# A Mamba stage in an eight-stage kernel: gate, norm and softplus moved between engines

## The chip, the cores and the metric

One core of one Trainium2 chip (trn2) runs the whole program in one launch. The metric is the device time of an execution in microseconds. The engines meant here are TensorE (PE, with PEld for its weight loads), VectorE (DVE), ScalarE (ACT), GpSimd (POOL) and SyncE (SP), which mostly issues DMAs. Each has its own queue of instructions and runs it in order; they meet at semaphores.

## The reference

The program is a decoder of four layers on x of shape (4, 256, 256), each layer a cross-attention and a feed-forward block with gated residuals. Only the first block, a Mamba layer, is touched by the change:

```
def _L0_xattn_ref(hidden_states, z, in_proj_w, conv_w, conv_b, x_proj_w, dt_proj_w, dt_proj_b, A_log, D):
    x = einsum('bld,ed->bel', hidden_states, in_proj_w)
    xc = conv_general_dilated(x, conv_w, padding=[(3, 0)], feature_group_count=256)
    x = silu(xc + conv_b[None, :, None])
    dt_low, Bm, Cm = split(einsum('bdl,ed->bel', x, x_proj_w), [8, 24], axis=1)
    dt = softplus(einsum('brl,dr->bdl', dt_low, dt_proj_w) + dt_proj_b[None, :, None])
    A = -exp(A_log)                                  # 256 x 16
    state = state * exp(dt_t[..., None] * A) + (dt_t * u_t)[..., None] * B_t[:, None, :]   # scan over 256 steps
    y_t = einsum('bdn,bn->bd', state, C_t)
    y = (y + D[None, :, None] * x) * silu(z)
    return swapaxes(y, 1, 2)

x = x + tanh(g_xattn[0]) * _L0_xattn_ref(ctx_1024, _layernorm(x), ...)
x = x + tanh(g_ffn[0]) * _L0_ffn_ref(_layernorm(x), ...)
...
```

So the gate z is the layer norm of x, and the block's result is added to x, of which the next norm is taken for the dense feed-forward block.

## The kernel before

The 1024 tokens are eight tiles (t, NT = 8) of 128 tokens for everything that has tokens on the partitions (X, xn, gate), and two halves (h) of 512 tokens for everything that has channels on the partitions. There are 256 inner channels, two chunks (c, NI = 2) of 128. The state has 16 components; one component of one half is a unit s (UNITS = 32: units 0 to 15 are half 0, 16 to 31 half 1).

Each engine's program is written out by hand, one function for each engine (`mamba_pe`, `mamba_act`, `mamba_dve`, `mamba_pool`, `mamba_sp`); the order in the function is the order in the engine's queue. `tick` and `at` name the semaphore value of an event: an instruction ticks it, others wait for it.

Ahead of the loop: VectorE makes the convolution's weights (L707) and the statistics of x (`bn_stats`, `bn_aggr`, and a small add, "var", L232), for tiles 0 to 3 and then 4 to 7. GpSimd makes 1/sqrt of them by a power (`deviation_pool`, L239), behind a large cast (`sel`, L401). TensorE runs the convolution of half 0 (L440), ScalarE its silu, U (L556), TensorE the projection (L451), ScalarE copies its lowest rows (`low`, L563), TensorE makes dt (L460) and ScalarE and VectorE the softplus: ScalarE Abs (L570), Exp (L575), Ln (L579), VectorE relu (L661), 1 + e (L666), the remainder of that rounding (L671), V minus it (L674), the sum (L679, "DT") and the product with U (L682, "DU"). Meanwhile VectorE splits the projection's rows into three bf16 parts (`split`).

In the loop, each unit s: TensorE spreads a row of B and one of C over the partitions (`rows_of`, L475), ScalarE copies C (L605), in odd units B as well (L601), and makes dA = exp(A dt) into PSUM (L610); VectorE multiplies DU by B (L728; in odd units GpSimd does chunk 1, L410) and scans (L735); GpSimd multiplies the scan by C (L418), and TensorE adds that into y (`add`, L481). One-off work is put behind certain units by `if s == ...` in each engine's loop: half 1's convolution (units 0 to 3) on TensorE; the norms of x, xn (`norm_dve`, L246), on VectorE behind units 0 and 1; silu of half 1 and the gate (L617) on ScalarE at unit 4; the split behind units 6 and 7; half 1's softplus in units 8 to 11; tanh at 11; gating, transposing and adding the first half's result in units 17 to 19; the statistics for the dense stage (tag "d") behind 19, their power on GpSimd in unit 20, the norms on VectorE behind 21, their transposes (`turn_pe`, L258) in 22 and the copies (`turned_act`, `turned_dve`) in 23. The dense stage (L807) starts when TensorE is through with Mamba.

An activation of another function set needs an ACT_TABLE_LOAD; `table_act` runs a dummy activation so that the load comes early. `deviation_dve` and `norm_dve` serve other stages too. GpSimd's loop is:

```
    for s in range(m.UNITS):
        if s + 1 < m.UNITS and shared_out(s + 1):
            ...  # multiply for unit s + 1, chunk 1
        for c in range(m.NI):
            ...  # HC(s, c)
        if s == 20:
            deviation_pool(k, "d", 0)
```

## Time and profile before

| | |
|---|---|
| median of 3 runs | 1137.84 us (1134.45 to 1142.14) |
| profiled execution | 1136.88 us, span 1135.6 us |
| instructions in the span | 14899 |
| busy: PE / DVE / ACT / POOL | 949.6 / 730.4 / 519.2 / 300.4 us |
| chain that ended last | PE 59%, DVE 15%, ACT 3% of the span |
| mean granted TensorE clock | 0.925 of full speed |

The profiled execution is one run, and its span is measured from its first to its last instruction; 1.28 us lie around it. Busy time says how much an engine did, not whether it held up others: for that one reads the chain, or the wait that ended last at a place. Mamba takes the first 174 us of the span.

### The profile page before, as it was taken

How to read it: one execution, taken by the hardware profiler on the slowest of the kernel's cores; microseconds unless marked ns; L12 is line 12 of the kernel's file. 1: busy time of each engine (PE TensorE's matmuls, PEld its weight loads, DVE VectorE, ACT ScalarE, POOL GpSimd, SP SyncE). 2: the span in 40 equal slices, each digit the busy share in tenths (PEclk: the TensorE clock that was granted, in tenths of full speed). 3: DMA queues.
4: the chain of work that ended last, by engine and by line, in shares of the span. 5: the costliest groups of instructions: out<-in, count | busy, mean ns of one | idle time of the engine just before them, and what ended most of it. 6: DMA issues, size and time to landing. Idle time of an engine off the chain costs nothing.

```text
span 1135.6 us, 14899 instructions
## 1 busy us (share of the span) xinstructions
PE 949.6 (84%) x4834; PEld 679.5 (60%) x4834; DVE 730.4 (64%) x1864; ACT 519.2 (46%) x1330; POOL 300.4 (26%) x281
## 2 busy tenths in 40 slices
PE   5677679999999999999997798865878788976556
PEld 2222234668999998888975576733545555544445
DVE  5899994335666668687665346557677855567653
ACT  3574461136666665665632343443356542132331
POOL 3477791131111112143105204341222100010110
PEclk9887899999999999999999799987789999989678
DMA  8400001011111172113004246220100003211100
GB/s 313 201 1 0 1 0 46 1 42 29 43 43 33 43 260 98 43 63 100 11 20 168 74 139 195 94 89 15 43 1 1 1 2 134 74 40 38 70 19 19
DMA packets 28356, 73.96 MB, mean 65 GB/s; under 512 B 4076, under 2 KB 5366, under 8 KB 27640
## 3 DMA queue, kind: packets, MB, share of 16 engines
q1 hardware_dynamic: 24344, 63.28, 16.2%
q0 software_dynamic: 3072, 8.39, 2.3%
q10 hardware_dynamic: 864, 1.34, 0.3%
q8 instruction: 40, 0.66, 0.2%
q14 instruction: 36, 0.29, 0.1%
HBM read 50.98 MB, written 22.02 MB: 64 GB/s over the span
## 4 chain that ended last, share of the span: by engine, by line
PE 59%; DVE 15%; ACT 3%; issue 3%; another core or an unknown queue 2%; POOL 1%; SPq 1%; DMA 1%; DVEq 0%; POOLq 0%; ACTq 0%
PE psum L2042 5%; PE psum L946 5%; PE psum L1652 4%; PE psum L1138 4%; PE psum L1149 4%; PE psum L807 4%; PE psum L1118 4%; PE psum L949 3%; PE psum L1666 2%; PE psum L1129 2%; DVE arena L2338 2%; PE psum L818 2%; PE psum L970 2%; PE psum L2061 2%
## 5 line engine op out<-in xcount | busy, mean ns | idle before, releaser
L1028 POOL TENSOR_TENSOR arena<-arena,mhalf 128x8 f32<-128x8 f32 x32 | 53.7, 1678 | 258.5 <-DVE arena L1013 258.5
L1250 DVE SCALAR_TENSOR_TENSOR X<-psum,arena,X 128x256 f32<-128x256 f32 x128 | 55.9, 478 | 66.7 <-PE psum L1149 64.5
L418 POOL TENSOR_TENSOR arena<-arena 128x512 f32<-128x512 f32 x64 | 83.5, 1331 | 7.4 <-DVE arena L735 4.2
L735 DVE TENSOR_TENSOR_SCAN arena<-psum,arena 128x512 f32<-128x512 f32 x64 | 74.6, 1207 | 3.3 <-ACT psum L610 1.8
L1192 ACT ACTIVATE arena<-psum,arena 128x256 f32<-128x256 f32 x128 | 60.0, 477 | 34.9 <-DVE arena L1229 34.7
L481 PE MATMUL psum<-arena,ident 128*128 128x512 f32 x128 | 72.3, 690 | 1.1 <-POOL arena L418 0.8
L1652 PE MATMUL psum<-arena 128*128 x248 | 66.4, 391 | 7.4 <-DVE arena L1747 4.0
L1758 DVE COPY arena<-psum 128x256 f32<-128x256 f32 x62 | 26.2, 422 | 64.5 <-PE psum L1666 55.3
L1149 PE MATMUL psum<-arena 128*128 128x256 f32 x256 | 65.9, 380 | 1.2 <-DVE X L1250 1.1
L1138 PE MATMUL psum<-arena 128*128 128x256 f32 x256 | 66.5, 383 | 0.0
L2323 ACT ACTIVATE arena<-psum,arena 128x240 f32<-128x240 f32 x128 | 57.4, 465 | 19.1 <-DVE arena L2343 14.6
L1118 PE MATMUL psum<-arena 128*128 128x256 f32 x256 | 65.8, 380 | 0.0
L946 PEld LDWEIGHTS psum<-arena,xT 128*128 128x128 f32 x512 | 62.0, 192 | 1.5
L946 PE MATMUL psum<-arena,xT 128*128 128x128 f32 x512 | 62.3, 275 | 0.0
L2042 PE MATMUL psum<-xT,arena 128*128 128x512 f32 x128 | 60.8, 615 | 1.3 <-ACT arena L3095 1.2
L239 POOL TENSOR_TENSOR rstd<-rstd,mhalf 128x4 f32<-128x4 f32 x16 | 16.3, 1019 | 164.3 <-DVE rstd L232 164.2
L475 PE MATMUL psum<-arena 96*128 96x512 bf16 x64 | 22.4, 436 | 41.7 <-DVE arena L728 41.5
L984 ACT ACTIVATE arena<-psum 128x512 f32<-128x512 f32 x64 | 38.3, 598 | 35.9 <-PE psum L946 17.8
L1204 ACT COPY arena<-psum 128x512 f32<-128x512 f32 x64 | 37.6, 588 | 34.5 <-PE psum L1129 34.4
L1118 PEld LDWEIGHTS psum<-arena 128*128 128x128 f32 x256 | 48.2, 190 | 6.6 <-issue 0.3
L1652 PEld LDWEIGHTS psum<-arena 128*128 128x128 f32 x248 | 43.1, 194 | 14.2 <-issue 10.8
L1149 PEld LDWEIGHTS psum<-arena 128*128 128x128 f32 x256 | 46.3, 190 | 7.0 <-issue 1.4
(348 smaller groups left out, 2282.5 us busy)
## 6 DMA issues: line engine op xcount, KB each, us to landing
arena<-in_w SPq DMA_DIRECT2D x32, 384.0 KB
tokens<-arena SPq DMA_DIRECT2D x2, 4096.0 KB, 23.0
arena<-tokens SPq DMA_DIRECT2D x32, 256.0 KB
results<-arena SPq DMA_DIRECT2D x32, 256.0 KB
arena<-in_moe SPq DMA_DIRECT2D x17, 384.0 KB, 3.0
arena<-in_moe SPq DMA_DIRECT2D x4, 1536.0 KB, 13.8
arena<-in_w SPq DMA_DIRECT2D x2, 1024.0 KB, 6.6
arena<-in_gu SPq DMA_DIRECT2D x1, 1280.0 KB, 5.9
```

Source lines behind the costliest of these rows:

```text
L418: nc.gpsimd.tensor_tensor(m.HC[:, v, :], m.Hs[:, v, :], m.Cs[:, s % 2, :], ALU.mult).then_inc(*tick("HC", s, c))
L481: nc.tensor.matmul(bank[m.bank_Y[h][c]], k.ident[:, :], m.HC[:, 2 * (s % 2) + c, :], start=False, stop=n == NSTATE - 1).then_inc(*tick("y_ ...
L735: nc.vector.tensor_tensor_scan(m.Hs[:, 2 * (s % 2) + c, :], bank[m.bank_dA[c]], input_of(m, s, c), 0.0, ALU.mult, ALU.add).then_inc(*tick( ...
L946: mm = nc.tensor.matmul(bank[b][:, j * P:(j + 1) * P], k.xT[:, c, t * P:(t + 1) * P], m.W[:, p, c * P:(c + 1) * P], start=c == 0, stop=c = ...
L1118: mm = nc.tensor.matmul(bank[w][:, j * S:(j + 1) * S], m.Q[:, N % 2, i * S + j * P:i * S + (j + 1) * P], m.K[:, N % 2, i * S:(i + 1) * S], ...
L1138: mm = nc.tensor.matmul(bank[4][:, 0:S], m.ctok[:, 2 * m.batch(u) + c, :], m.PT[:, u % 2, c, :], start=c == 0, stop=c == 1)
L1149: mm = nc.tensor.matmul(bank[5][:, j * D:(j + 1) * D], m.Z[:, u % 2, j * P:(j + 1) * P], m.M[:, h, :], start=True, stop=True)
L1192: e = nc.scalar.activation(m.Pr[:, w, j, :], bank[w][:, j * S:(j + 1) * S], ACT.Exp, bias=m.nb[:, w, j:j + 1], scale=m.SCALE, accum_out=m. ...
L1250: a = nc.vector.scalar_tensor_tensor(k.X[:, t, :], bank[5][:, j * D:(j + 1) * D], m.ri[:, u % 4, j:j + 1], k.X[:, t, :], ALU.mult, ALU.add)
L1652: mm = nc.tensor.matmul(bank[b][:, 0:D], m.xgT[:, n % 2, c, :], m.W[:, bass.ds(place + c * D, D)], start=c == 0, stop=c == DC - 1)
L2042: mm = nc.tensor.matmul(bank[b], m.W[:, slot, which, c * P:(c + 1) * P], k.xT[:, c, cols], start=c == 0, stop=c == DC - 1)
L2323: nc.scalar.activation(pr[:, a, 0:KM], v[:, a, 0:KM], ACT.Exp, bias=m.nb[:, u, a:a + 1], scale=m.SCALE, accum_out=m.sums[:, a % 2, places[ ...
```

## The change

- ScalarE makes the gate straight from X, tile by tile, silu(x * rstd + shift) with shift = -mean * rstd, in the start: six tiles between the two silus of half 0 and two behind them. VectorE's eight norms behind units 0 and 1 go. The statistics of all eight tiles are finished in one go; GpSimd's power is on 8 columns and stands ahead of its large cast.
- The next norm (tag "d", tiles 0 to 3) is made by ScalarE behind units 21 and 22 from a `shift` that VectorE makes behind unit 20; transposes and copies move from 22 and 23 to 24 and 25.
- The rectification of softplus moves from VectorE to ScalarE (Relu).
- Exp and Ln are used from one table set, loaded once behind `low` and once behind half 1's silu. Tanh moves from unit 11 to the very start, with the DMAs of `ident` and `rows` ahead of those of the projection weights.
- Softplus works chunk by chunk; in half 0 the remainder of chunk 1 is made by GpSimd in three instructions. Half 1's steps are spread over units 8 to 14.

```diff
 # constants_act
     nc.scalar.dma_start(k.cols[:, :], k.io["cols"]).then_inc(*landed("cols_in"))
+    nc.scalar.dma_start(k.ident[:, :], k.io["ident"]).then_inc(*landed("ident_in"))
+    nc.scalar.dma_start(k.rows[:, :], k.io["rows"].partition_broadcast(P)).then_inc(*landed("rows_in"))
     nc.scalar.dma_start(m.Wx, k.io["x_proj"]).then_inc(*landed("Wx_in"))
     nc.scalar.dma_start(m.Wdt[96:96 + m.RANK], k.io["dt_proj"]).then_inc(*landed("Wdt_in"))
-    nc.scalar.dma_start(k.ident[:, :], k.io["ident"]).then_inc(*landed("ident_in"))
-    nc.scalar.dma_start(k.rows[:, :], k.io["rows"].partition_broadcast(P)).then_inc(*landed("rows_in"))
 # mamba_pool
+    pool.wait_ge(*at("var", "m"))
+    nc.gpsimd.tensor_tensor(k.rstd[:, :], k.rstd[:, :], k.mhalf[:, 0:NT], ALU.pow).then_inc(*tick("rstd", "m"))
     pool.wait_ge(*at("sel", 1))
     nc.gpsimd.tensor_copy(m.sel, m.row.unsqueeze(2).broadcast_to([P, n, P])).then_inc(*tick("sel", 2))
-    for h in range(2):
-        deviation_pool(k, "m", h)
+
+    pool.wait_ge(*at("sp_1", 0, 1))
+    nc.gpsimd.tensor_scalar(m.HC[:, 3, :], m.DT[:, 0, 1, :], -1.0, None, ALU.add).then_inc(*tick("sp_ep", 0))
+    pool.wait_ge(*at("sp_ep", 0))
+    nc.gpsimd.tensor_tensor(m.E[:, 1, :], m.HC[:, 3, :], m.E[:, 1, :], ALU.subtract).then_inc(*tick("sp_ep", 1))
+    pool.wait_ge(*at("sp_ep", 1))
+    pool.wait_ge(*at("rectified", 0, 1))
+    nc.gpsimd.tensor_tensor(m.E[:, 1, :], m.V[:, 1, :], m.E[:, 1, :], ALU.subtract).then_inc(*tick("sp_vp"))
 # mamba_pe
-            pe.wait_ge(*at("relu", 0, 0))
+            pe.wait_ge(*at("rectified", 0, 0))
...
-        elif s == 22:
+        elif s == 24:
             k.free[4], k.free[5] = [("x_m", 0)], [("x_m", 1)]
-            turn_pe(k, "d", 0, (4, 5))
+            turn_pe(k, "d", 0, (4, 5), "xn_a")
 # mamba_act
-    table_act(k, ACT.Silu, "m_silu")
+    def gate(tiles):
+        act.wait_ge(*at("shift", "m"))
+        for t in tiles:
+            a = nc.scalar.activation(m.gate[:, t, :], k.X[:, t, :], ACT.Silu, scale=k.rstd[:, t:t + 1],
+                                     bias=k.shift[:, t:t + 1])
+        if t == NT - 1:
+            a.then_inc(*tick("gate"))
+    def rectified(h, c):
+        nc.scalar.activation(m.V[:, c, :], bank[m.bank_dt[h][c]], ACT.Relu,
+                             bias=k.col("dt_b", c)).then_inc(*tick("rectified", h, c))
+    def norm(t):
+        act.wait_ge(*at("shift", "d", t // HT))
+        nc.scalar.activation(k.xn[:, t, :], k.X[:, t, :], ACT.Identity, scale=k.rstd[:, t:t + 1],
+                             bias=k.shift[:, t:t + 1]).then_inc(*tick("xn_a", "d", t))
+
+    table_act(k, ACT.Tanh, "m_tanh")
+    act.wait_ge(*at("rows_in"))
+    nc.scalar.activation(k.tg[:, :], k.row("g"), ACT.Tanh).then_inc(*tick("tg"))
+    table_act(k, ACT.Silu, "m_silu", (("idle", "m_tanh"),))
     act.wait_ge(*at("cols_in"))
+    silu(0, 0)
+    gate(range(0, 6))
+    silu(0, 1)
+    gate(range(6, NT))
+    low(0)
+    nc.scalar.preload_act_table_set("natural_log_exp_and_others")
     for c in range(NI):
-        silu(0, c)
-    low(0)
-    magnitude(0)
-    exponential(0)
+        magnitude(0, c)
+        exponential(0, c)
+    for c in range(NI):
+        rectified(0, c)
+        logarithm(0, c)
...
-    logarithm(0)
-    table_act(k, ACT.Exp, "m_exp")
...
         if s == 4:
             for c in range(NI):
                 silu(1, c)
-            act.wait_ge(*at("xn", "m", NT - 1))
-            nc.scalar.activation(m.gate, k.xn[:, :, :], ACT.Silu).then_inc(*tick("gate"))
+            nc.scalar.preload_act_table_set("natural_log_exp_and_others")
...   # magnitude at 8, then rectified at 9, exponential at 10, logarithm at 11, each for both chunks
-            act.wait_ge(*at("rows_in"))
-            nc.scalar.activation(k.tg[:, :], k.row("g"), ACT.Tanh).then_inc(*tick("tg"))
-        elif s == 23:
+        elif s in (21, 22):
+            for t in range(2 * (s - 21), 2 * (s - 20)):
+                norm(t)
+        elif s == 25:
             turned_act(k, "d", 0, (4, 5))
 # mamba_dve
-    for h in range(2):
-        for t in range(4 * h, 4 * h + 4):
-            stats_dve(k, "m", t, (f"x_in{h}",))
-        deviation_dve(k, "m", h)
+    for t in range(NT):
+        stats_dve(k, "m", t, (f"x_in{t // HT}",))
+    for t in range(NT):
+        dve.wait_ge(*at("bn_stats", "m", t))
+        a = nc.vector.bn_aggr(k.mv[:, t, :], k.stats[:, t, :])
+    a.then_inc(*tick("bn_aggr", "m"))
+    dve.wait_ge(*at("bn_aggr", "m"))
+    nc.vector.tensor_scalar(k.rstd[:, :], k.mv[:, :, 1], 1e-5, None, ALU.add).then_inc(*tick("var", "m"))
+    dve.wait_ge(*at("rstd", "m"))
+    nc.vector.scalar_tensor_tensor(k.shift[:, :], k.mv[:, :, 0], -1.0, k.rstd[:, :], ALU.mult,
+                                   ALU.mult).then_inc(*tick("shift", "m"))
     split(0, range(5))
-    dve.wait_ge(*at("cols_in"))
     for c in range(NI):
-        relu(0, c)
+        plus_one(0, c)
+    remainder(0, 0)
+    softplus(0, 0)
     dve.wait_ge(*at("A_exp"))
     nc.vector.tensor_scalar(m.A, m.A, -1.0, None, ALU.mult).then_inc(*tick("A"))
-    plus_one(0)
-    remainder(0)
-    softplus(0)
+    softplus(0, 1)
...
-        if s < 2:
-            norm_dve(k, "m", s)
-        elif s == 6:
+        if s == 6:
...
-        elif s == 8:
+        elif s == 10:
             for c in range(NI):
-                relu(1, c)
-        elif s == 9:
-            plus_one(1)
-        elif s == 10:
-            remainder(1)
-        elif s == 11:
-            softplus(1)
+                plus_one(1, c)
+        elif s in (11, 12):
+            remainder(1, s - 11)
+        elif s in (13, 14):
+            softplus(1, s - 13)
...
-        elif s == 21:
-            norm_dve(k, "d", 0)
-        elif s == 23:
+        elif s == 20:
+            shift_dve(k, "d", 0)
+        elif s == 25:
             turned_dve(k, "d", 0, (4, 5))
```

`shift_dve` is in the kernel before already, for later stages:

```
def shift_dve(k, tag, h):
    half = slice(HT * h, HT * h + HT)
    k.dve.wait_ge(*k.s.at("rstd", tag, h))
    k.nc.vector.scalar_tensor_tensor(k.shift[:, half], k.mv[:, half, 0], -1.0, k.rstd[:, half], ALU.mult,
                                     ALU.mult).then_inc(*k.s.tick("shift", tag, h))
```

## Rows read from the trace of the kernel before

**Rows 1.** Busy time by stretch: PE, PEld, DVE, ACT, POOL, then PEclk, DMA share, GB/s.

```profile
31.60:170.30 138.70, 101.21 (x229) 40.00 (x230) 129.69 (x151) 78.98 (x126) 102.15 (x80) 0.86 0.08 32
...
174.30:1135.60 961.30, 828.65 (x4570) 632.72 (x4570) 581.19 (x1674) 427.40 (x1188) 185.24 (x181) 0.93 0.19 62
```

**Rows 2.** The chain of waits to 230 us: start us, us, what.

```profile
175.40 10.30 PE psum L807 x24
```

**Rows 3.** Timeline of the start: start us, us, engine, line, operation [idle before <-releaser].

```profile
10.88 3.60 POOL L401 CAST arena<-arena 128x4096 bf16<-128x4096 f32 x1
...
11.58 2.92 DVE L232 TENSOR_SCALAR rstd<-mv 128x4 f32<-128x4 f32 x1
...
13.23 0.33 SPq L788 DMA_DIRECT2D arena<-in_gu  x1
...
14.41 1.39 DVE L222 BATCH_NORM_STATS2 stats<-X 128x6 f32<-128x256 f32 x4
...
17.89 0.69 ACT L556 ACTIVATE arena<-psum,cols 128x512 f32<-128x512 f32 x1 [2.68 <-PE psum L440]
...
19.77 0.58 ACT L563 COPY arena<-psum 8x512 f32<-8x512 f32 x1 [1.20 <-PE psum L451]
...
23.19 1.28 ACT L575 ACT_TABLE_LOAD   x1
...
31.61 1.28 DVE L728 TENSOR_TENSOR arena<-arena,psum 128x512 f32<-128x512 f32 x2
```

**Rows 4.** Single lines' instructions: duration ns min/median/max, first and last start us.

```profile
L1028 POOL TENSOR_TENSOR arena<-arena,mhalf x32: 1637/1638/2542, 233.5 to 559.1; 128x8 f32<-128x8 f32 x32
...
L2961 ACT ACTIVATE xn<-X,shift,rstd x8: 584/596/602, 994.8 to 1105.4; 128x256 f32<-128x256 f32 x8
...
L653 DVE TENSOR_TENSOR arena<-arena x2: 687/687/687, 22.7 to 70.1; 96x512 f32<-96x512 f32 x2
...
L671 DVE SCALAR_TENSOR_TENSOR arena<-arena x2: 1226/1534/1843, 26.5 to 84.2; 128x1024 f32<-128x1024 f32 x2
...
L418 POOL TENSOR_TENSOR arena<-arena x64: 1262/1272/2244, 35.5 to 171.0; 128x512 f32<-128x512 f32 x64
```

**Rows 5.** Groups by line and form, DVE, 31.6 to 56 us: busy us, mean ns.

```profile
L246 DVE TENSOR_SCALAR xn<-X,mv,rstd 128x256 f32<-128x256 f32 x8 | 5.9, 792 | 0.0
```

**Rows 6.** Timeline of the loop's first units, PE, ACT and DVE.

```profile
41.11 2.97 PE L440 MATMUL psum<-arena 128*128 128x512 f32 x4
...
47.29 1.88 PE L440 MATMUL psum<-arena 128*128 128x512 f32 x4
...
51.16 1.88 PE L440 MATMUL psum<-arena 128*128 128x512 f32 x4
...
54.28 1.91 ACT L617 ACTIVATE arena<-xn 128x2048 f32<-128x2048 f32 x1
...
59.19 1.22 DVE L735 TENSOR_TENSOR_SCAN arena<-psum,arena 128x512 f32<-128x512 f32 x1 [1.80 <-ACT psum L610]
```

**Rows 7.** Groups by line and form, DVE, 84 to 95 us: busy us, mean ns.

```profile
L674 DVE TENSOR_TENSOR arena<-arena 128x1024 f32<-128x1024 f32 x1 | 2.2, 2171 | 0.0
L682 DVE TENSOR_TENSOR arena<-arena 128x1024 f32<-128x1024 f32 x1 | 2.2, 2168 | 0.0
L671 DVE SCALAR_TENSOR_TENSOR arena<-arena 128x1024 f32<-128x1024 f32 x1 | 1.8, 1843 | 0.0
L679 DVE TENSOR_TENSOR arena<-arena 128x1024 f32<-128x1024 f32 x1 | 1.4, 1400 | 0.0
```

**Rows 8.** Timeline of the loop's middle, DVE.

```profile
75.70 1.38 DVE L661 TENSOR_SCALAR arena<-psum,cols 128x512 f32<-128x512 f32 x2
...
102.96 1.28 DVE L728 TENSOR_TENSOR arena<-arena,psum 128x512 f32<-128x512 f32 x2 [1.67 <-PE psum L475]
```

**Rows 9.** Timeline around units 20 and 21, POOL and DVE.

```profile
133.17 1.00 POOL L239 TENSOR_TENSOR rstd<-rstd,mhalf 128x4 f32<-128x4 f32 x1
...
134.21 3.26 DVE L246 TENSOR_SCALAR xn<-X,mv,rstd 128x256 f32<-128x256 f32 x4 [0.64 <-POOL rstd L239]
```

More of the change, by code:

```diff
@@ L247, in norm_dve, with turn_pe @@
                                   ALU.subtract, ALU.mult).then_inc(*k.s.tick("xn", tag, t))
-def turn_pe(k, tag, h, banks):
+def turn_pe(k, tag, h, banks, made="xn"):
     for b in banks:
@@ L255, in turn_pe @@
         t = HT * h + j
-        k.pe.wait_ge(*k.s.at("xn", tag, t))
+        k.pe.wait_ge(*k.s.at(made, tag, t))
         for c in range(DC):
@@ L563, in low @@
         nc.scalar.copy(m.low[96:96 + m.RANK, :], bank[m.bank_x[h]][96:96 + m.RANK, :]).then_inc(*tick("low", h))
-    def magnitude(h):
-        for c in range(NI):
-            act.wait_ge(*at("dt_ps", h, c))
-            if h:
-                act.wait_ge(*at("sp_v", 0))
-            nc.scalar.activation(m.E[:, c, :], bank[m.bank_dt[h][c]], ACT.Abs,
-                                 bias=k.col("dt_b", c)).then_inc(*tick("abs", h, c))
-    def exponential(h):
-        act.wait_ge(*at("abs", h, 1))
-        nc.scalar.activation(m.E, m.E, ACT.Exp, scale=-1.0).then_inc(*tick("sp_exp", h))
@@ L577, in logarithm @@
-    def logarithm(h):
-        act.wait_ge(*at("sp_1", h))
-        nc.scalar.activation(m.DU[:, h], m.DT[:, h], ACT.Ln).then_inc(*tick("ln", h))
-    table_act(k, ACT.Silu, "m_silu")
-    act.wait_ge(*at("cols_in"))
-    for c in range(NI):
-        silu(0, c)
-    low(0)
-    magnitude(0)
-    exponential(0)
+    def gate(tiles):
[5 more added lines that the diff above has]
+            a.then_inc(*tick("gate"))
@@ new lines, in magnitude, with exponential @@
+    def magnitude(h, c):
+        act.wait_ge(*at("dt_ps", h, c))
+        if h:
+            act.wait_ge(*(at("sp_vp") if c else at("sp_v", 0, 0)))
+        nc.scalar.activation(m.E[:, c, :], bank[m.bank_dt[h][c]], ACT.Abs,
+                             bias=k.col("dt_b", c)).then_inc(*tick("abs", h, c))
+    def rectified(h, c):
+        nc.scalar.activation(m.V[:, c, :], bank[m.bank_dt[h][c]], ACT.Relu,
+                             bias=k.col("dt_b", c)).then_inc(*tick("rectified", h, c))
+    def exponential(h, c):
+        act.wait_ge(*at("abs", h, c))
+        nc.scalar.activation(m.E[:, c, :], m.E[:, c, :], ACT.Exp, scale=-1.0).then_inc(*tick("sp_exp", h, c))
@@ new lines, in logarithm @@
+    def logarithm(h, c):
+        act.wait_ge(*at("sp_1", h, c))
+        nc.scalar.activation(m.DU[:, h, c, :], m.DT[:, h, c, :], ACT.Ln).then_inc(*tick("ln", h, c))
+    def norm(t):
[5 more added lines that the diff above has]
+    nc.scalar.activation(k.tg[:, :], k.row("g"), ACT.Tanh).then_inc(*tick("tg"))
@@ L620, in mamba_act @@
         elif s == 8:
-            magnitude(1)
+            for c in range(NI):
+                magnitude(1, c)
         elif s == 9:
-            exponential(1)
+            for c in range(NI):
+                rectified(1, c)
         elif s == 10:
-            logarithm(1)
+            for c in range(NI):
+                exponential(1, c)
         elif s == 11:
-            act.wait_ge(*at("rows_in"))
-            nc.scalar.activation(k.tg[:, :], k.row("g"), ACT.Tanh).then_inc(*tick("tg"))
-        elif s == 23:
+            for c in range(NI):
+                logarithm(1, c)
+        elif s in (21, 22):
+            for t in range(2 * (s - 21), 2 * (s - 20)):
+                norm(t)
+        elif s == 25:
             turned_act(k, "d", 0, (4, 5))
```

53 lines of the change are left out of this document (25 added, 28 removed).

## The prediction, made before the changed kernel ran

> **What bounds the kernel now.** I read the page for the span, then the stretches, then the chain of waits near 174 us, then the timeline of the Mamba stage engine by engine. Only Mamba is edited. Behind it TensorE is nearly always busy (828.65 us of 961.30), while in Mamba's loop it is VectorE: 129.69 us of 138.70 [rows 1]. The first dense matmul starts at 175.40, straight behind Mamba's last steps [rows 2], so a microsecond saved or lost at Mamba's end should pass whole to the kernel's end. What the change takes from VectorE inside the loop therefore counts, as long as no other engine becomes late there. The stage's start, 0 to 31.61 us, is a chain from engine to engine and can lose as well.
>
> **The start: the gate now stands in front of the second silu.** ScalarE's queue becomes silu(0,0), six gate tiles, silu(0,1), two gate tiles, low(0). All gate tiles wait for `shift`, which needs the statistics of all eight tiles. When can it be there? The second half of x lands at 13.2 us, for SyncE's next issue, which waits for it, is at 13.23. Four statistics take 1.39 us [rows 3], to 14.65; eight aggregations and the small add I estimate at 0.9: 15.5. GpSimd's power on 128x8 takes 1.64 us [rows 4]: 17.2. Behind it in GpSimd's queue stands the cast that makes `sel`, 3.60 us, until 20.8. In the trace VectorE's small add, started at 11.58 beside that cast, took 2.92 us and ended at 14.50, when the cast did (14.48) [rows 3]. Here GpSimd has its cast ready the moment the power ends, while VectorE must first see the semaphore, so I take `shift` to lose the race and finish at 20.9. One gate tile is of the form of L2961, 0.59 us alone and by my estimate 0.50 in a row; six take 3.1: 24.0. silu(0,1), which began at 17.89 [rows 3], then begins 6.1 us late. The second projection matmul runs after a long idle of TensorE, and loses up to 0.8 if it gets the lower level (two conv taps took 2.97 us at 41.11 and 1.88 at 47.29) [rows 6]. I take a delay of 6.5 us. Its bounds: 2.6 if `shift` is not blocked (17.4 + 3.1 = 20.5 against 17.89), 6.9 at most.
>
> The Trainium skill (SBUF — State Buffer, "Who interferes with whom") says that a VectorE instruction with two SBUF inputs and a GpSimd instruction that reads SBUF exclude each other, and that issue order decides who blocks. It speaks against both GpSimd steps of this change, the cast behind the power and the softplus chunk. The 2.92 us row agrees for an add; for the two-input `shift` no row here shows it beside a cast. By the rule the sum is the one below, without it that of rivals 1 and 2.
>
> Tanh moves to the front of ScalarE's queue, where it waits for `rows`, whose transfer is now issued third instead of fifth; the projection weights move behind it. Neither costs anything here: behind tanh and its table load of 1.28 come silu(0,0) and then the gate's wait until 20.9 (17.4 in the first rival), which leaves several microseconds of cover. Without that cover it would be at most the load, 1.3.
>
> **The start: softplus.** From low (19.77) to the first loop multiply (31.61) it was 11.84 us [rows 3]. Gone from this chain: two table loads of 1.28, as one set, loaded while TensorE makes dt, serves Exp and Ln; two rectifications of VectorE, 1.4 us as in the loop [rows 8]. Added: chunks, which pay an overhead each (a 512-wide two-input operation takes 0.69 and a 1024-wide one 1.23), and three GpSimd operations, of which two take 1.27 as in the loop and the third, a scalar add of the same width, I put at 1.3 too [rows 4]. From low: VectorE's split ends at 4.0; plus_one twice 4.95; then VectorE's remainder and the three GpSimd operations want the same port. If they exclude each other as in [rows 7], the order is VectorE 0.6, GpSimd 1.3, VectorE 0.6, GpSimd 1.2, and so on: GpSimd is done at 10.3, VectorE's last product at 12.2. If not, it is done near 9.8. I take +0.3, nearer to the blocked end since the loop's rows show blocking; bounds -2.0 and +0.4.
>
> **The loop's first units.** VectorE loses its eight norms, 5.9 us [rows 5], and at unit 5 ScalarE loses the gate of 1.91, behind which VectorE waited, 1.80 ahead of the scan alone [rows 6]; the table loads stay two. VectorE alone would gain 5.9 + 1.9 = 7.8. But TensorE becomes late instead: in units 0 to 3 it has rows, adds and four half convolutions. From 33 us it would be gapless: its waits of some 2.3 us for VectorE go. From there each unit costs it 3.87 us as before (47.29 to 51.16) [rows 6]. conv(1,1) ends near 50.7 instead of 53.04; then silu 0.69, a load 1.28, two copies and the exponential: the scan of unit 5 starts at 54.4 instead of 59.19. Gain 4.8; bounds 4.0 and 6.0 (if the clock is up a unit earlier).
>
> **The loop's middle.** Two rectifications leave VectorE: -1.3 (1.38 with the overlap of the next) [rows 8], and ScalarE takes them in unit 9 with idle time to spare. The stall of 1.67 ahead of 102.96 [rows 8], when TensorE was late with a row behind the skip matmuls, is now covered by a softplus chunk: -1.7 (0 to 1.7). The remainder and softplus were four 1024-wide operations of 1.84, 2.17, 1.40 and 2.17 us, 7.5 with the overlap [rows 7], against 4 x 1.23 = 4.9 unblocked, and GpSimd's products beside them took up to 2.24 instead of 1.27 [rows 4]. Eight 512-wide ones in four pairs need 1.3 a pair, and each pair meets GpSimd again: half an operation on entry and up to a whole one between. I take 1.2 of wait a pair, as the two old pairs had 1.5 and 1.1: 4 x 2.5 = 10.0, so +2.5. Bounds: no wait, 5.2, so -2.3; the full 1.9 each, 12.8, so +5.3.
>
> **The next norm.** It goes to ScalarE, and `shift` is put behind unit 20 where norms stood behind unit 21. But `rstd` is still made by GpSimd behind its products of unit 20, 133.17 to 134.17. VectorE was through with unit 21 at 133.57, waited 0.64 and worked 3.26 [rows 9]. With unit 21 costing it 3.0, it comes to the end of unit 20 at 130.6, and now waits 3.6 there, with unit 21's multiply and scans queued behind the waiting `shift`, and GpSimd's and TensorE's share of unit 21 waiting for those. Unit 22 then starts at 137.3 instead of 137.4: 0.1 gained, not 3.8. Bounds 0 and -3.8 (if GpSimd, less locked by now, were 3.6 us earlier). Transposes and copies move two units later, beside work that has room until the dense stage; no cost.
>
> **The sum** against the profiled execution, 1136.88 (span 1135.6 and 1.28 around it; the median of the runs is 1137.84, a tenth of a per cent above): +6.5 + 0.3 - 4.8 - 1.3 - 1.7 + 2.5 - 0.1 = +1.4, so 1138.3, rounded to 1138.
>
> **The rivals.**
> 1. `shift` is not blocked by the cast. For: it reads only eight columns and may win; against: the add of 2.92 us. Delay 2.6: 1134.4.
> 2. The chunks slip between GpSimd's work, at both places (-2.3, -2.0 for +2.5, +0.3): -7.1, so 1131.2. For: GpSimd is idle in parts of units 10 to 14; against: its products are queued whenever a scan ends. With rival 1: 1127.3.
> 3. The table set isn't kept: Exp and Ln get loads of their own. For: in the trace Exp sits behind a load of its own, 23.19 [rows 3]. Against: the preload names the set. Three loads of 1.28 (Exp, Ln, Exp again) then stand in the start's chain, 0.3 of them covered: +3.5, so 1141.8.
> 4. Slower: VectorE and GpSimd lock each other for the whole of units 10 to 14, at the full 1.9 a pair, while TensorE's lower level holds the first units to 4.0: +2.8 + 0.8, so 1141.9. It decides once GpSimd has a product waiting at every chunk; above 1% only if GpSimd, thus late, drags the following units by 8 us more. Against: it caught up in units 14 to 16 before.
>
> **How the numbers follow.** Forecast 48%, rival 1 15%, rival 2 with or without 1 15%, rival 3 7%, rival 4 15%. A measurement of this kernel can't tell less than about 1% (11.4 us) from no change. Faster by that needs below 1126.5: rivals 1 and 2 together with a short first part, 13%. Slower by that is the far end of 4, 6%; the same 81%. The range 1128 to 1144 takes in 1131 to 1142 with the bounds of the single terms.
>
> **What would show it.** `shift` ending with the cast near 20.9 and silu(0,1) near 24; low near 26.3; the loop's first multiply near 38; unit 5's scan near 61; chunks of remainder and softplus above 1 us each; a wait of about 3.6 us on `rstd` behind unit 20; the first dense matmul near 176.8. I am wrong if silu(0,1) starts before 21, if that wait is short, or if dense matmuls don't shift with Mamba's end.

## The result and the profile after

The changed kernel takes 1141.49 us (median; 1137.95 to 1145.72) where the kernel before, on the same chips, takes 1138.03 (1134.45 to 1142.80), 20 runs of each. The ratio is 1.0031 with a 95% interval of 1.0018 to 1.0043: about 3.5 us more (2 to 5 by the interval, which leaves out no difference at all), and well inside the 1% that the prediction called no change. The time lies in the range; the place of nearly every microsecond is another question, and the traces answer it.

I read the stretches first. The columns are the stretch, its length, the busy time of PE, PEld, DVE, ACT and POOL, then TensorE's granted clock, DMA share and GB/s. The last two lines answer to [rows 1]; the first two are two pieces of the start.

```profile
23.80:25.60 1.80, 1.07 (x2) 0.22 (x3) 0.01 (x1) 1.57 (x4) 0.00 (x0) 1.00 1.03 426
25.63:29.30 3.67, 3.67 (x4) 1.12 (x4) 3.35 (x7) 2.48 (x3) 0.00 (x0) 0.50 1.03 426
...
31.60:170.30 138.70, 100.30 (x230) 39.23 (x228) 128.66 (x149) 79.58 (x135) 103.88 (x81) 0.86 0.07 30
177.43:1138.30 960.87, 831.47 (x4564) 634.48 (x4562) 581.48 (x1674) 427.65 (x1188) 185.30 (x181) 0.94 0.18 62
```

The part behind Mamba is 960.9 us long, and was 960.4 before: the dense matmul at the head of the chain's piece [rows 2] starts at 175.24 in TensorE's timeline, and the span ended at 1135.6. Now it starts at 177.43. So Mamba ends 2.2 us later, and that is what needs an explanation. The stretch from 31.60 takes in the last 6 us of the changed kernel's start, so its 128.66 us of VectorE can't be compared with 129.69. From the first multiply to the end of the last scan VectorE is busy 124.87 us of 134.63 (37.79 to 172.42), where it was 129.69 of 138.62: the loop itself is 4.0 us shorter, with 4.8 us less work for VectorE, and the start has lost more than that.

By the ratio it is 3.5. A single trace may say less, for two reasons. `shift` starts 3.94 to 3.95 us behind the landing of x's second half (SyncE's next issue) in all eleven traces of the changed kernel and its variants, and that landing varies: 12.55 in this one, 13.51 in the repeat below, where the dense matmuls start at 178.88. And the part behind Mamba took from 957.4 to 964.0 us in the seven later traces near 1137 us. So the starts inside Mamba say more than the end of a trace.

So I go through Mamba by the start of the same step in both traces. "Step" is what this stretch itself lost or won.

| first start of | before | after | late by | step |
|---|---|---|---|---|
| silu(0,1) on ScalarE | 17.89 | 23.04 | +5.15 | +5.15 |
| low(0) | 19.77 | 24.91 | +5.14 | 0.0 |
| loop's first multiply | 31.61 | 37.79 | +6.18 | +1.04 |
| unit 5's scan | 59.19 | 58.31 | -0.88 | -7.06 |
| unit 8's scan | 73.45 | 74.25 | +0.80 | +1.68 |
| unit 9's scan | 77.76 | 77.25 | -0.51 | -1.31 |
| unit 16's scan | 110.82 | 113.03 | +2.21 | +2.72 |
| unit 20's scan | 128.24 | 130.46 | +2.22 | 0.0 |
| unit 22's multiply | 137.39 | 139.54 | +2.15 | -0.1 |
| first dense matmul | 175.24 | 177.43 | +2.19 | 0.0 |

The timeline of the changed kernel's start answers to [rows 3] (start us, duration, engine, line, operation, [idle before <-releaser]; from four engines):

```profile
9.53 1.43 DVE L740 TENSOR_TENSOR arena<-arena 128x256 f32<-128x256 f32 x4 [8.66 <-DMA arena<-in_conv_taps]
...
14.80 1.67 POOL L401 TENSOR_TENSOR rstd<-rstd,mhalf 128x8 f32<-128x8 f32 x1 [8.55 <-DVE rstd L748]
...
16.42 3.60 POOL L403 CAST arena<-arena 128x4096 bf16<-128x4096 f32 x1
...
16.50 3.54 DVE L750 SCALAR_TENSOR_TENSOR shift<-mv,rstd 128x8 f32<-128x8 f32 x1 [1.79 <-POOL rstd L401]
...
20.08 3.06 ACT L576 ACTIVATE arena<-X,shift,rstd 128x256 f32<-128x256 f32 x6 [2.90 <-DVE shift L750]
23.04 0.67 ACT L564 ACTIVATE arena<-psum,cols 128x512 f32<-128x512 f32 x1
...
24.91 0.58 ACT L571 COPY arena<-psum 8x512 f32<-8x512 f32 x1 [0.21 <-PE psum L459]
25.50 1.28 ACT L615 ACT_TABLE_LOAD   x1
```

To be seen: GpSimd goes from the power straight into the cast (16.42), VectorE's `shift`, eight columns wide, begins 0.08 us later and ends with it, at 20.04; ScalarE's next idle time, 2.90, is named for `shift`; and one table load stands where Exp and Ln had loads of their own. TensorE's timeline and VectorE's at unit 5 answer to [rows 6]:

```profile
23.77 1.10 PE L459 MATMUL psum<-arena 128*104 128x512 f32 x2 [3.08 <-ACT arena L564]
...
25.63 3.74 PE L468 MATMUL psum<-arena 8*128 8x512 f32 x4 [0.76 <-ACT arena L571]
...
39.95 3.24 PE L448 MATMUL psum<-arena 128*128 128x512 f32 x4
...
44.32 1.88 PE L448 MATMUL psum<-arena 128*128 128x512 f32 x4
...
52.06 1.88 PE L448 MATMUL psum<-arena 128*128 128x512 f32 x4
...
57.23 0.69 DVE L767 TENSOR_TENSOR arena<-arena,psum 128x512 f32<-128x512 f32 x1 [2.75 <-ACT arena L633]
58.31 2.34 DVE L774 TENSOR_TENSOR_SCAN arena<-psum,arena 128x512 f32<-128x512 f32 x2 [0.39 <-ACT psum L642]
```

The four matmuls of the timestep take 3.74 us, against 1.95 in the trace of before (the first line below), and the granted clock of that stretch is 0.50, the lower level of 1.2 GHz: TensorE had idled 3.08 us ahead of the two matmuls in front of them. In the loop it is the other way round: the second of the four half convolutions, slow before [rows 6], runs at 2.4 GHz, for TensorE no longer idles in the unit before it.

```profile
20.50 1.95 PE L460 MATMUL psum<-arena 8*128 8x512 f32 x4 [0.76 <-ACT arena L563]
```

VectorE's timeline of the middle answers to [rows 7] and [rows 8], the last two lines, of POOL and DVE, to [rows 9]:

```profile
83.20 2.89 DVE L698 TENSOR_SCALAR arena<-arena 128x512 f32<-128x512 f32 x2
...
89.03 0.86 DVE L703 SCALAR_TENSOR_TENSOR arena<-arena 128x512 f32<-128x512 f32 x1
89.93 1.64 DVE L707 TENSOR_TENSOR arena<-arena 128x512 f32<-128x512 f32 x1
...
102.78 1.27 DVE L767 TENSOR_TENSOR arena<-arena,psum 128x512 f32<-128x512 f32 x2
...
135.35 1.04 POOL L239 TENSOR_TENSOR rstd<-rstd,mhalf 128x4 f32<-128x4 f32 x1
...
136.43 0.16 DVE L2982 SCALAR_TENSOR_TENSOR shift<-mv,rstd 128x4 f32<-128x4 f32 x1 [3.64 <-POOL rstd L239]
```

Each pair of softplus chunks takes 2.5 us (89.03 to 91.57, and 2.4, 2.5 and 2.6 for the other three); the stall ahead of unit 14 is gone, yet the unit starts at 102.78, only 0.18 earlier; and the add of 1, once one operation of 0.86, is two of together 2.89. Behind unit 20 VectorE waits 3.64 us for `rstd`.

### The profile page after: what moved, and what is told of

The parts are those of the page before. It is cut to its first block, busy times and chain, and to the rows that moved or that the text cites. A ratio compares the mean times of both kernels' runs of the same rounds, so it can differ in the third digit from the quotient of the medians.

```text
span 1138.3 us, 14912 instructions
## 1 busy us (share of the span) xinstructions
PE 954.9 (84%) x4834; PEld 682.6 (60%) x4834; DVE 726.8 (64%) x1857; ACT 522.4 (46%) x1346; POOL 303.8 (27%) x283
## 4 chain that ended last, share of the span: by engine, by line
PE 60%; DVE 15%; ACT 3%; another core or an unknown queue 3%; issue 3%; POOL 1%; DVEq 0%; POOLq 0%
PE psum L981 5%; PE psum L2077 5%; PE psum L1173 5%; PE psum L1184 4%; PE psum L1153 4%; PE psum L1687 4%; PE psum L842 4%; PE psum L984 3%; PE psum L1164 2%; PE psum L1005 2%; PE psum L853 2%; PE psum L1701 2%; DVE arena L2373 2%; PE psum L2096 2%
## 5 line engine op out<-in xcount | busy, mean ns | idle before, releaser
L1153 PEld LDWEIGHTS psum<-arena 128*128 128x128 f32 x256 | 48.2, 190 | 6.6 <-issue 0.3
L1687 PEld LDWEIGHTS psum<-arena 128*128 128x128 f32 x248 | 43.4, 196 | 14.1 <-issue 10.7
L2697 PE MATMUL psum<-ident,arena 128*128 128x128 f32 x256 | 39.1, 300 | 15.0 <-ACT arena L2360 10.8
```

Of the source, the lines that this page charges most:

```text
L1153: mm = nc.tensor.matmul(bank[w][:, j * S:(j + 1) * S], m.Q[:, N % 2, i * S + j * P:i * S + (j + 1) * P], m.K[:, N % 2, i * S:(i + 1) * S], ...
L1687: mm = nc.tensor.matmul(bank[b][:, 0:D], m.xgT[:, n % 2, c, :], m.W[:, bass.ds(place + c * D, D)], start=c == 0, stop=c == DC - 1)
```

## The experiments

The first four ran on a chip on which the stages behind Mamba are faster (kernel before: 1106.67 us) and Mamba the same, the other seven on two chips with the times of before near 1137. So I compare ratios, each with its own before, and starts of steps inside Mamba.

**What `shift` behind the cast costs.** The cast needs nothing of the norm; it is put ahead of the wait for the variance.

```diff
+    pool.wait_ge(*at("sel", 1))
+    nc.gpsimd.tensor_copy(m.sel, ...)            # the cast
     pool.wait_ge(*at("var", "m"))
     nc.gpsimd.tensor_tensor(k.rstd[:, :], ..., ALU.pow).then_inc(*tick("rstd", "m"))
-    pool.wait_ge(*at("sel", 1))
-    nc.gpsimd.tensor_copy(m.sel, ...)
```

> The changed kernel with GpSimd's large cast put ahead of its wait for var. My theory (shift lost 3.5 us to the cast's hold on the shared port, and all ScalarE work behind the gate waits for it): shift takes about 0.2 us and ends at 16.7, the gates begin at 17.1 behind silu(0,0), silu(0,1) at 20.2 instead of 23.04, low near 22.0, the first dense matmul near 174.5 instead of 177.43; time 1138.6, ratio to the kernel before 1.0005. Rival (the shift was slow for another reason, such as its own form or the power before it): shift still takes 3.5 us, ratio 1.003. Second rival (a saving in the start is taken up by later stalls of the loop): the first dense matmul stays near 177.

Measured: ratio 0.9982 (0.9971 to 0.9994), so 5.4 us less than the changed kernel's 1.0031 makes of it. Timeline of this kernel, POOL, DVE and PE:

```profile
6.16 3.60 POOL L401 CAST arena<-arena 128x4096 bf16<-128x4096 f32 x1
...
16.42 0.17 DVE L750 SCALAR_TENSOR_TENSOR shift<-mv,rstd 128x8 f32<-128x8 f32 x1 [1.79 <-POOL rstd L403]
...
22.17 1.95 PE L468 MATMUL psum<-arena 8*128 8x512 f32 x4 [0.76 <-ACT arena L571]
...
32.96 1.28 DVE L767 TENSOR_TENSOR arena<-arena,psum 128x512 f32<-128x512 f32 x2
...
172.64 10.47 PE L842 MATMUL psum<-xT,arena 128*128 128x512 f32 x24
```

`shift` takes 0.17 instead of 3.54. The first multiply comes 4.83 earlier and the dense matmul 4.79, more than the block itself: TensorE's idle ahead of the projection's second part is 0.26 instead of 3.08, and the timestep is back at 1.95. One badly placed cast cost the block, 3.5 at silu(0,1), and behind `low` 1.4 us more. That this part is TensorE's clock the other traces bear out: from `low` to the first multiply it is 11.5 us where the timestep takes 1.95, 12.3 where it takes 3.20 (`shift` behind unit 21), 12.65 at 3.52 (the repeat) and 12.9 at 3.74. This is the rule of the Trainium skill (SBUF — State Buffer, "Who interferes with whom") on the read port that GpSimd and VectorE's second input share, and it holds for an operation of eight columns as for a wide one.

**Whether the new order of ScalarE's transfers is free.** Identity matrix and broadcast rows are issued behind the projection weights again.

```diff
-    nc.scalar.dma_start(k.ident[:, :], k.io["ident"])...
-    nc.scalar.dma_start(k.rows[:, :], k.io["rows"].partition_broadcast(P))...
     nc.scalar.dma_start(m.Wx, ...)
     nc.scalar.dma_start(m.Wdt[96:96 + m.RANK], ...)
+    nc.scalar.dma_start(k.ident[:, :], ...)
+    nc.scalar.dma_start(k.rows[:, :], ...)
```

> The changed kernel with the DMAs of ident and rows put back behind the projection weights. In the changed kernel the convolution taps landed 1.14 us later than before, and x's second half 0.7 us earlier. Theory A (the start hangs on shift alone): the convolution starts at 8.96 again, but x lands at 13.2 and shift, the gates and silu(0,1) come 0.7 us later; first dense matmul near 178.1, ratio 1.004. Theory B (the start hangs on the convolution): 1.1 us gained, first dense matmul near 176.3, ratio 1.002. If the DMA order has no part in the landings, taps stay at 9.5.

Measured: ratio 1.0023 (1.0013 to 1.0033). Line of its timeline, DVE:

```profile
8.14 1.55 DVE L740 TENSOR_TENSOR arena<-arena 128x256 f32<-128x256 f32 x4 [7.28 <-DMA arena<-in_conv_taps]
```

The taps land 1.4 us earlier than in the changed kernel. In the seven traces with the rows early the wait for them ended at 9.4 to 10.6, in the six with the rows late at 7.7 to 8.4. But `shift`, which waits for all of x, sets the end, and x's second half lands at 12.86 against 12.55. That the order moves x is not shown: it landed at 12.5 to 13.6 with the rows early and at 12.6 to 13.2 with them late. The first multiply comes at 39.01, 1.22 later, and the dense matmul at 178.32. Of the 1.22, x accounts for 0.3; the other 0.9 is TensorE's. Its convolution now ends earlier while silu(0,1) doesn't, so it idles 5.36 us instead of 3.08, and already the projection's second part runs at the lower clock, 2.03 us for 1.10, with 0.50 granted:

```profile
24.06 2.03 PE L459 MATMUL psum<-arena 128*104 128x512 f32 x2 [5.36 <-ACT arena L564]
```

So the order of transfers is not free for the taps, but that is hidden behind the statistics of x; and earlier taps alone only lengthened TensorE's idle time, so that taking the order back by itself gains nothing. With the cast first as well, below, that idle is 1.20 and the projection takes 1.11.

**The wait on `rstd`.** The next norm's `shift` stands behind unit 21 instead of 20, its tiles on ScalarE one unit later.

```diff
-        elif s == 20:
+        elif s == 21:
             shift_dve(k, "d", 0)
...
-        elif s in (21, 22):
-            for t in range(2 * (s - 21), 2 * (s - 20)):
+        elif s in (22, 23):
+            for t in range(2 * (s - 22), 2 * (s - 21)):
```

> The changed kernel with the shift of the next norm put behind unit 21 and ScalarE's norms behind 22 and 23. Theory (VectorE's 3.64 us wait on rstd behind unit 20 was paid whole, because VectorE bounds the loop): a wait of 0.5 us is left, the first dense matmul comes at 174.4 instead of 177.43, time 1138.5, ratio 1.0004. Rival (GpSimd used the wait to catch up, and without it VectorE waits elsewhere in units 21 to 31, or the transposes come late): less than 1 us gained, ratio 1.0025 or more.

Measured: ratio 0.9985 (0.9967 to 1.0003), dense matmul at 175.58, 1.85 earlier; 2.2 with this trace's first multiply at 38.12, 0.33 later, taken off. Its timeline, POOL and DVE:

```profile
135.50 1.04 POOL L239 TENSOR_TENSOR rstd<-rstd,mhalf 128x4 f32<-128x4 f32 x1
136.51 2.50 POOL L426 TENSOR_TENSOR arena<-arena 128x512 f32<-128x512 f32 x2
...
136.57 1.22 DVE L2982 SCALAR_TENSOR_TENSOR shift<-mv,rstd 128x4 f32<-128x4 f32 x1 [0.86 <-POOL rstd L239]
```

The wait shrinks from 3.64 to 0.86, as expected. The missing 1 us is in the last line: `shift` now comes as GpSimd goes from the power into its next product, and takes 1.22 instead of 0.16. The start's race again, at another place.

**The three together.**

> The three edits together. If the first and the third are independent and the second shifts x by 0.7 us: silu(0,1) near 20.4, first dense matmul near 171.8, time 1135.8, ratio 0.998. If they are not (one saving hides the other): above 1138, ratio above 1.000.

Measured: ratio 0.9959 (0.9944 to 0.9974), dense matmul at 171.16. The gains add up, for all three together give 6.3 us against the changed kernel's trace: 4.8 are the cast's and 2.0 the norm's place, less the 0.5 by which this trace's first multiply (33.50) is behind that of the cast alone. The result of "no change" is thus a sum of removable losses and a gain of nearly the same size.

**The changed kernel once more,** as the partner of the next three on another chip, unedited.

> The changed kernel as it is, beside the kernel before and the next three on one chip. Earlier runs were on a chip whose later stages are faster. All theories: Mamba as in the profile after (first dense matmul near 177.4), ratio 1.003.

Measured: ratio 1.0029 (1.0011 to 1.0048), first multiply 38.51, dense matmul 178.88. The second half of x landed at 13.51 here and the wait for the taps ended at 10.5.

**Softplus of half 1 at full width.** Each pair of 512-wide chunks is one 1024-wide operation on VectorE; ScalarE's Ln and exponentials and the loop's multiplies wait for the whole instead of a chunk (these waits are left out below).

```diff
-            for c in range(NI):
-                plus_one(1, c)              # behind unit 10
-        elif s in (11, 12):
-            remainder(1, s - 11)
-        elif s in (13, 14):
-            softplus(1, s - 13)
+            plus_one_whole()
+        elif s == 11:
+            remainder_whole()
+        elif s == 13:
+            softplus_whole()
```

> The changed kernel with half 1's softplus on VectorE in 1024-wide operations again (1 + e behind unit 10, the remainder behind 11, sum and product behind 13). Theory (each narrow operation on VectorE pays for GpSimd's product anew: the ten took 13.0 us, 2.89 for 1 + e and 2.4 to 2.7 a pair, against 8.3 for the five wide ones before): 4.7 us gained, less up to 1.7 if TensorE's stall ahead of unit 14 returns; first dense matmul between 172.7 and 174.4 instead of 177.43; ratio 0.999 to 1.0005. Rival (the lock's total is the same, only spread): first dense matmul within 1 us of 177.4.

Measured: ratio 0.9995 (0.9980 to 1.0011), dense matmul at 174.25, 4.63 earlier than in the repeat. From the first multiply to the dense matmul it gains 4.4 against the repeat and 3.7 against the first trace of the changed kernel, where 3.0 to 4.7 were expected. Its timeline, DVE:

```profile
83.23 1.75 DVE L698 TENSOR_SCALAR arena<-arena 128x1024 f32<-128x1024 f32 x1
...
87.91 1.73 DVE L702 SCALAR_TENSOR_TENSOR arena<-arena 128x1024 f32<-128x1024 f32 x1
89.67 2.17 DVE L705 TENSOR_TENSOR arena<-arena 128x1024 f32<-128x1024 f32 x1
...
98.21 2.21 DVE L710 TENSOR_TENSOR arena<-arena 128x1024 f32<-128x1024 f32 x1
100.45 1.22 DVE L713 TENSOR_TENSOR arena<-arena 128x1024 f32<-128x1024 f32 x1
```

Five operations of 9.1 us do what ten of 13.0 did (83.20's 2.89 and four pairs of 2.4 to 2.6): in the ten, the second of each pair took 1.64 where it takes 0.69 undisturbed, for it met GpSimd's product anew. The stall ahead of unit 14 doesn't come back: with rectification on ScalarE, and the softplus behind unit 13, its cover remains.

**No GpSimd in the start's softplus.** Chunk 1 of half 0 goes back to VectorE.

```diff
-    pool.wait_ge(*at("sp_1", 0, 1))
-    nc.gpsimd.tensor_scalar(m.HC[:, 3, :], m.DT[:, 0, 1, :], -1.0, ...)
-    ...                                     # and the two subtractions on GpSimd
     nc.vector.tensor_scalar(m.A, m.A, -1.0, None, ALU.mult).then_inc(*tick("A"))
+    remainder(0, 1)
     softplus(0, 1)
```

> The changed kernel with the remainder of half 0's second chunk on VectorE, GpSimd's three instructions gone. Theory (GpSimd's three took 5.1 us in the start and VectorE's waited for them in turn): VectorE's ten steps run back to back, the first loop multiply comes near 36.4 instead of 37.79, first dense matmul near 176.0, ratio 1.0018. Rival (GpSimd's share is a real relief, as two narrow operations leave VectorE's queue): first loop multiply at 38.4 or later, ratio 1.0035.

Measured: ratio 1.0017 (1.0000 to 1.0034), which the repeat's interval does not exclude. From chunk 1's add of 1 to the first multiply it is 6.1 us, against 7.0 with GpSimd: 0.9 gained. But the first multiply is only 0.17 earlier and the dense matmul, at 178.63, 0.25. What went missing ahead of chunk 1 is 0.7: x landed 0.11 later, and TensorE, which had idled 3.68 us for 2.94, took 1.47 for 1.10 over the projection's second part and 3.75 for 3.52 over the timestep. In the loop VectorE has new waits for ScalarE, 0.16 in unit 2 and twice 0.4 in unit 3. The chunk on GpSimd is worth a little less than nothing: VectorE would have done it in 1.4 us, and lost 2.2 in locks.

**The gate at its old place, straight from x.** Its eight tiles leave the start and stand behind silu(1,·) at unit 4.

```diff
     silu(0, 0)
-    gate(range(0, 6))
     silu(0, 1)
-    gate(range(6, NT))
...
                 silu(1, c)
+            gate(range(NT))
```

> The changed kernel with all eight gate tiles, still straight from x, at unit 4 instead of around the second silu. Theory (the gate costs its place whichever it is): silu(0,1) at 19.7, low near 21.6, the first loop multiply 4.3 us earlier at 33.5, but VectorE's stall at unit 5 grows by the eight tiles' 4.1: first dense matmul near 177.2, ratio 1.003. Rival (the loop hides the gate, since ScalarE is idle 40% of it): first dense matmul near 173.5, ratio 0.9995.

Measured: ratio 1.0037 (1.0021 to 1.0053), first multiply 33.46, dense matmul 177.31. Its timeline, ACT and DVE at unit 5:

```profile
51.04 4.03 ACT L576 ACTIVATE arena<-X,shift,rstd 128x256 f32<-128x256 f32 x8
...
57.00 0.69 DVE L766 TENSOR_TENSOR arena<-arena,psum 128x512 f32<-128x512 f32 x1 [6.66 <-ACT arena L631]
```

The start is 5.05 us shorter than in the repeat, and VectorE pays 3.9 of it back in one wait of 6.66 where it had 2.75. ScalarE has two places at which others wait for it, and the gate's 4 us cost about the same at either. This trace keeps 1.6 us at the dense matmul, the ratio shows none of it: which of the two places is better can't be told by these intervals.

**The gate from x as the only change.** The kernel before, with the gate in eight tiles from x at unit 4 and VectorE's eight norms [rows 5] left out; in the start VectorE makes two small `shift`s instead, 0.15 us each.

```diff
-            act.wait_ge(*at("xn", "m", NT - 1))
-            nc.scalar.activation(m.gate, k.xn[:, :, :], ACT.Silu)...
+            act.wait_ge(*at("shift", "m", 1))
+            for t in range(NT):
+                a = nc.scalar.activation(m.gate[:, t, :], k.X[:, t, :], ACT.Silu, scale=..., bias=...)
...
+    for h in range(2):
+        shift_dve(k, "m", h)
...
-        if s < 2:
-            norm_dve(k, "m", s)
```

> The kernel before with one part of the change alone: the gate stays at unit 4 but is made straight from x in eight tiles on ScalarE, and VectorE's eight norms of 5.9 us are removed. Theory (TensorE does not become late when VectorE's norms go; what is late is ScalarE, by the 2.1 us that eight tiles take longer than one wide gate): of a lead of 5.3 us at unit 4 about 3.2 us are gained, the first dense matmul comes at about 172.1 us against 175.2, and the ratio is about 0.997. Rival (my forecast's reading, TensorE is late next, with a lead of 2.3 to 3.0 us before the slower gate): the gain is at most 0.9 us, the first dense matmul comes at 174.3 us or later, and the ratio is 0.999 or more.

Measured: ratio 0.9989 (0.9972 to 1.0006), dense matmul at 173.34. Its timeline, PE, ACT and DVE:

```profile
37.63 1.88 PE L440 MATMUL psum<-arena 128*128 128x512 f32 x4
...
45.37 1.88 PE L440 MATMUL psum<-arena 128*128 128x512 f32 x4
...
46.05 1.28 ACT L556 ACT_TABLE_LOAD   x1
47.34 1.26 ACT L556 ACTIVATE arena<-psum,cols 128x512 f32<-128x512 f32 x2
...
53.03 0.69 DVE L733 TENSOR_TENSOR arena<-arena,psum 128x512 f32<-128x512 f32 x1 [5.24 <-ACT arena L601]
```

From the first multiply to unit 5's scan it is 24.47 us, against 27.58 before: 3.1 gained where 3.2 were expected and my forecast's reading allowed 0.9. TensorE's last half convolution ends at 47.25 and ScalarE's load of the table at 47.33: TensorE holds nobody up, though by only 0.08. Of the 3.1 (and 0.56 of an earlier first multiply in this trace) 1.9 are left at the dense matmul: units 6 to 8 give back 1.0, the stall ahead of unit 14 is 1.09 instead of 1.67, 0.6 more gained, the wait for `rstd` behind unit 21 costs 0.2 more, and a wait of 0.99 for TensorE's transposes ahead of unit 24 is new. The ratio's 1.2 us is less than I expected, and its interval takes in no change.

**All edits that helped.** The changed kernel with the cast first, the broadcast rows (not the identity matrix) issued late, `shift` behind unit 21, softplus of half 1 at full width and no GpSimd chunk.

> The changed kernel with five edits at once: the cast stands ahead of the wait for the variance, the identity matrix stays early but the broadcast rows are issued behind the projection weights, the next norm's scale and shift stand behind unit 21, softplus half 1 is whole-width on VectorE and ScalarE, and no chunk of it is on GpSimd. Theory (the costs found so far are places in one chain and add up): the first dense matmul of the kernel with the three moves came at 171.16 us; less 4.15 us for the whole-width softplus and 0.8 us for the GpSimd chunk it comes at about 166.2 us, against 175.24 before, and the ratio of times to before is about 0.992 (9 us less of about 1138). The taps land at about 8.3 us if the rows alone delay them, at 9.4 us or later if the identity matrix does. Rival (the gains overlap: once half 1 is shorter ScalarE is late for units 14 to 16, or TensorE is): the first dense matmul comes at 168.5 us or later and the ratio is 0.994 or more.

Measured: 1129.47 us (1127.32 to 1131.13) against 1136.85, ratio 0.9931 (0.9912 to 0.9951). Its timeline, DVE and PE:

```profile
8.33 2.57 DVE L752 TENSOR_TENSOR arena<-arena 128x256 f32<-128x256 f32 x4 [7.45 <-DMA arena<-in_conv_taps]
...
32.83 1.28 DVE L780 TENSOR_TENSOR arena<-arena,psum 128x512 f32<-128x512 f32 x2
...
53.94 2.34 DVE L787 TENSOR_TENSOR_SCAN arena<-psum,arena 128x512 f32<-128x512 f32 x2 [0.39 <-ACT psum L635]
...
166.45 10.47 PE L854 MATMUL psum<-xT,arena 128*128 128x512 f32 x24
```

The sum stands: 166.45 for an expected 166.2, so Mamba ends 8.8 us ahead of the kernel before and 11 ahead of the changed one. And the taps are early though the identity matrix is too, here and in the next kernel (8.33 and 8.36): it is the broadcast rows that delay them. (The 2.57 us of the taps' four products, 1.5 before, are beside GpSimd's cast, which now runs there.)

**One step more.** In that kernel the Silu of half 1 and the table load behind it stand between unit 5's copies and its exponential.

```diff
+        if s == 5:                           # behind unit 5's copies of B and C
+            for c in range(NI):
+                silu(1, c)
+            nc.scalar.preload_act_table_set("natural_log_exp_and_others")
...
-        if s == 4:
-            for c in range(NI):
-                silu(1, c)
-            nc.scalar.preload_act_table_set("natural_log_exp_and_others")
```

> The kernel e8_combined with one more edit: the Silu of tile 1 and the table load behind it are moved from behind unit 4 to between unit 5's copies and its exponential. Theory (unit 5's first product waits 2.75 us for ScalarE's copies, which stand behind that Silu and the load of 1.28 us): the wait shrinks to under 1.5 us, unit 5's scan comes about 1.0 us earlier, the first dense matmul at about 165.2 us, ratio about 0.991. Rival (the scan waits for the exponential, which comes no earlier): unit 5's scan stands where it does in e8_combined within 0.3 us, and so does the first dense matmul.

Measured: 1127.70 us, ratio 0.9923 (0.9902 to 0.9944), but the trace says that the edit lost. Its timeline, ACT and DVE:

```profile
49.90 0.59 ACT L626 COPY arena<-psum 128x512 f32<-128x512 f32 x1 [1.48 <-PE psum L476]
50.99 1.28 ACT L557 ACT_TABLE_LOAD   x1
...
50.52 0.69 DVE L780 TENSOR_TENSOR arena<-arena,psum 128x512 f32<-128x512 f32 x1 [0.34 <-ACT arena L626]
...
55.59 2.34 DVE L787 TENSOR_TENSOR_SCAN arena<-psum,arena 128x512 f32<-128x512 f32 x2 [4.38 <-ACT psum L639]
```

The wait ahead of the multiply shrinks to 0.34, and it comes 2.3 us earlier, but the scan waits 4.38 and comes 1.65 later, and the dense matmul stands at 167.20. The copies now wait 1.48 us for TensorE with nothing to do, a gap that Silu and its table load had filled, and the exponential comes behind all of it. So my expectation held for the wait alone, and the rival, that nothing would change, was wrong too: the wait was moved, and lengthened. The two kernels' times don't differ by more than their intervals.

## Why the prediction was right, point by point

The forecast of 1138 against 1141.49, on a sum of +1.4 against +2.2 in the trace (2.7 with what the part behind Mamba added), is right as a whole. By its terms it owes something to luck: a gain and several losses were both too small.

1. *Gate ahead of silu(0,1), +6.5.* Mechanism right, and this was the step that decided: `shift` lost the race, ended at 20.04 (20.9 was predicted), and the cast in front removed it. Measured +5.14. The term was 1.4 too large: `shift` was through 0.9 earlier than I had it, 0.7 of it since x landed earlier, and the projection behind silu(0,1) was no slower (1.87 us from that Silu to low, 1.88 before). In the repeat, where x landed at 13.51, `shift` ended at 21.00 and silu(0,1) started at 24.00, as forecast. (The rows at 41.11 and 47.29 that priced the slower projection are of four matmuls, not two; its price of 0.8 is still near the 0.9 that late rows showed.)
2. *Softplus of the start, +0.3.* Measured +1.04. The slower level that I had put on the projection came at the timestep, 3.74 for 1.95 us, and only part of it was covered by the removed loads. So points 1 and 2 together: +6.8 predicted, +6.18 measured. The locks with GpSimd came as worked out; the small A, 32 columns, took 1.23 under one of them.
3. *First units, -4.8.* Measured -7.06, beyond the bound of 6.0. This is the step that was mis-sized, and with it "TensorE becomes late instead". Counted from the first multiply, conv(1,1) ended 5.3 us earlier (53.94 less 6.18, against 53.04), and I had it 2.3 earlier, at 50.7. TensorE's waits for VectorE between those half convolutions were 2.20 and 1.06, so 3.3 us went and not 2.3. The rest is the clock: no longer idle there, TensorE did the second half convolution in 1.88 for 2.97 and the two matmuls ahead of it in 1.02 for 1.68. The way on to the scan, 4.4 us, was then 0.7 longer than my 3.7. Which engine is late next is almost a draw: ScalarE's table load ended at 54.02, TensorE's convolution at 53.94, and in the kernel with the gate from x alone they were as near (47.33 and 47.25). There eight gate tiles on ScalarE then set the wait, while the last kernel, with the Silu moved away, waited 1.48 us for TensorE.
4. *Not priced at all: units 5 to 8, +1.7.* VectorE, no longer late itself, runs up against ScalarE: waits of 0.47 ahead of unit 6's scan and 0.39 ahead of the second split are new, and the split's casts and sums, more of them beside GpSimd's products, took some 0.6 longer.
5. *Rectification -1.3 and the stall ahead of unit 14 -1.7.* Measured -1.3, and the stall is gone.
6. *Chunks of half 1, +2.5.* Four pairs took 9.9 us (10.0 predicted). But I priced remainder and softplus and forgot `plus_one`, also split in two: 2.89 us where one took 0.86: +2.0. With the stall and the chunks that gives 2.0 + 2.4 - 1.7 = 2.7, the whole step up to unit 16. The whole-width version got most of both back, 3.7 to 4.4 us.
7. *Next norm, -0.1.* Right: a wait of 3.64 (3.6 predicted), 0.1 us gained at unit 22.
8. *New order of transfers "costs nothing".* Wrong as a statement on the taps, which came 1.1 us later (2.1 in the repeat), right for the end only since `shift` waits for x in any case.

Rival 1 (`shift` not blocked) is refuted by the 3.54 us row, rival 2 (chunks slip between) by pairs of 2.5, rival 3 (table set not kept) by a single load ahead of Exp and none ahead of Ln. Rival 4 had both halves wrong: pairs didn't wait the full 1.9, and TensorE's clock went the other way. That a loss nearly ate a gain was foreseen; that each was removable by itself only the experiments showed.

## What to carry to other kernels

A tiny operation that stands on a chain (here 128x8, 0.17 us) takes as long as the GpSimd operation that starts just ahead of it (3.54 us): look at what GpSimd has ready at the very moment when it signals, and put that work ahead of its wait. Splitting an operation in two for earlier starts costs more than the overhead when each half can be blocked anew, so price every split operation, the cheap ones too. Look at what an idle engine comes back to: the late rows fed TensorE earlier, ahead of a wait that stayed, and it idled longer and then did the projection in 2.03 us instead of 1.10. And when a gain is a matter of places in queues, list all places of the moved work at which someone waits for it: moving the gate or the Silu only changed who waited.
